# Causal self-attention of a four-layer kernel: the values of a head as the 32-column stationary operand, in bursts of four chunks, instead of the weights as a 128-column one

## The reference, cut to what matters

```python
h = _rms(x, n1_w)
heads = lambda w_: (h @ w_.T).reshape(B, T, HEADS, HD).transpose(0, 2, 1, 3)
q = _rms(heads(wq), qn_w);  k = _rms(heads(wk), kn_w);  v = heads(wv)
scores = jnp.einsum('bhqd,bhkd->bhqk', q, k) * HD ** (-0.5)
scores = jnp.where(causal[None, None], scores, -jnp.inf)
attn = jax.nn.softmax(scores, axis=-1)
ao = jnp.einsum('bhqk,bhkd->bhqd', attn, v).transpose(0, 2, 1, 3).reshape(B, T, C) @ wo.T
ao = ao.at[:, :, :M].set(0.0)
x = x + ao
```

## Time and profile before

| | |
|---|---|
| median of the runs | 1413.52 us (1412.07 to 1416.41, 3 runs) |
| profiled execution, own time | 1418.93 us |
| its span in the trace | 1417.1 us |
| TensorE matmul busy | 1156.5 us (82%) |
| TensorE weight loads busy | 943.7 us (67%) |
| VectorE busy | 935.8 us (66%) |
| ScalarE busy | 716.8 us (51%) |
| GpSimd busy | 582.7 us (41%) |

### The profile page before, as it was taken

One profiled execution on the slowest core, in us unless ns is written; L12 is line 12 of the kernel. 1 busy time (PEld: TensorE's weight loads), 2 busy tenths in 40 slices (PEclk: granted clock), 3 DMA queues, 4 the chain that ended last, 5 costly groups with the idle time before them and its releaser, 6 DMA issues. The chain is left out here.

```text
span 1417.1 us, 24304 instructions
## 1 busy us (share of the span) xinstructions
PE 1156.5 (82%) x6976; PEld 943.7 (67%) x6976; DVE 935.8 (66%) x2154; ACT 716.8 (51%) x1337; POOL 582.7 (41%) x588
## 2 busy tenths in 40 slices
PE   5978899998996899844999287359477499999997
PEld 2655688887884699843888155247356387878785
DVE  6657788885553577754665578547565676767775
ACT  3556666665543555442565266237353255555553
POOL 3316634341000232453333233436354166667664
PEclk9998999997997999965999699679777599999998
DMA  7999410100001300013110560122421263444443
GB/s 198 217 191 177 86 45 28 39 28 1 1 0 62 112 1 2 17 56 101 42 50 22 163 160 22 35 61 79 134 77 46 48 130 120 117 121 119 119 122 101
DMA packets 115311, 115.16 MB, mean 81 GB/s; under 512 B 17141, under 2 KB 82300, under 8 KB 115218
## 3 DMA queue, kind: packets, MB, share of 16 engines
q1 hardware_dynamic: 109250, 104.64, 31.4%
q0 software_dynamic: 4544, 8.47, 1.8%
q10 hardware_dynamic: 1424, 0.92, 0.2%
HBM read 74.44 MB, written 34.16 MB: 77 GB/s over the span
## 5 line engine op out<-in xcount | busy, mean ns | idle before, releaser
L3109 POOL TENSOR_TENSOR e_h<-e_h,e_gate 128x512 f32<-128x512 f32 x128 | 187.9, 1485 | 135.9 <-DVE e_h L3161 89.7
L3166 DVE TENSOR_TENSOR e_h_low<-e_h,e_h_high 128x512 fp32r<-128x512 f32 x132 | 117.5, 890 | 75.8 <-ACT e_h_high L3096 75.6
L3096 ACT ACTIVATE e_h_high<-e_h 128x512 fp32r<-128x512 f32 x132 | 83.5, 633 | 97.8 <-POOL e_h L3109 90.1
L2565 POOL DMA_INDIRECT sorted_y<-zT,e_zb x78 | 75.8, 972 | 128.8 <-DVE zT L2723 113.4
L3161 DVE TENSOR_TENSOR e_h<-e_s,e_ps_b 128x512 f32<-128x512 f32 x132 | 89.4, 678 | 13.2 <-ACT e_s L3081 9.0
L1716 PE MATMUL u_ps_o<-u_vaug,u_pT 128*128 128x72 f32 x768 | 97.7, 270 | 0.0
L550 POOL DMA_INDIRECT sorted<-w_rows,w_index x64 | 71.9, 1123 | 57.9 <-DVE w_index L456 28.0
L1716 PEld LDWEIGHTS u_ps_o<-u_vaug,u_pT 128*128 128x128 f32 x768 | 93.3, 192 | 0.9
L3081 ACT ACTIVATE e_s<-e_ps_a 128x512 f32<-128x512 f32 x132 | 77.8, 589 | 30.9 <-PE e_ps_a L2157 28.3
L1397 POOL TENSOR_TENSOR s_kbd<-s_keys,groupmask 96x512 fp32r<-96x512 f32 x64 | 65.2, 1039 | 59.7 <-DMA s_keys<-s_k 33.8
L1744 ACT ACTIVATE u_sm<-u_sm 128x512 f32<-128x512 f32 x96 | 60.5, 631 | 50.3 <-DVE u_sm L1772 49.7
(11 more groups left out here) (575 smaller groups left out, 3532.4 us busy)
## 6 DMA issues: line engine op xcount, KB each, us to landing
e_gate<-gates_by_expert SPq DMA_DIRECT2D x256, 128.0 KB, 3.1
sorted<-blank SPq DMA_DIRECT2D x2, 8775.0 KB, 77.9
a_q<-q_part SPq DMA_DIRECT2D x24, 256.0 KB, 6.9
w_raw<-in_L1w SPq DMA_DIRECT2D x24, 256.0 KB, 4.1
e_zb<-sorted SPq DMA_DIRECT2D x78, 65.0 KB, 1.8
w_rows<-sorted_y SPq DMA_DIRECT2D x16, 256.0 KB, 4.9
s_keys<-s_k SPq DMA_DIRECT2D x8, 384.0 KB, 3.5
s_qs<-s_q SPq DMA_DIRECT2D x16, 192.0 KB, 2.6
```

The lines of the kernel that those rows point to most:

```text
L2565: nc.gpsimd.indirect_dma_start(out=y_dram, out_offset=bass.IndirectOffsetOnAxis(ap=at, axis=0), in_=y[j % NY][:, :], in_offset=None, bound ...
L3096: nc.scalar.activation(h_parts[k % 3][0][:, :], h[k % 3][:, :], ACT.Copy).then_inc(high_ready, 1)
L3109: nc.gpsimd.tensor_tensor(h[c % 3][:, :], h[c % 3][:, :], gate[pair % SLOTS][:, :], ALU.mult)\
L3166: nc.vector.tensor_tensor(h_parts[k % 3][1][:, :], h[k % 3][:, :], h_parts[k % 3][0][:, :], ALU.subtract).then_inc(low_ready, 1)
```

## The change

The values of one head, padded to 32 columns (8 channels, a one, zeros), become the stationary operand and the transposed weights `pT` of a block the moving one (128 columns). Head h writes output partitions 32 x (h mod 4) and following, columns 128 x (h div 4) and following, of `ps_o`. The products of four chunks (a set of 16 blocks) are issued together, at steps 6, 10 and 2 of the next batch, so `pT` becomes a ring of six. The result is now channels x queries, so ScalarE copies the bank (`oT`, 128x512), TensorE turns it back in four transposes two steps on, and VectorE divides what comes back. The finishing steps move on by three, and the loop has eleven steps behind it instead of eight.

```diff
-    NA = 8 * HD + 8
     CH = 12
+    SET = 4
+    RING = 6
+    WIDE = 32
-        vaug = [m.sb(f"vaug{i}", [P, 2, 8 * (NA + HD)]) for i in range(2)]
+        vaug = [m.sb(f"vaug{i}", [P, HEADS, WIDE]) for i in range(2)]
-        pT = [m.sb(f"pT{i}", [P, 4, P]) for i in range(2)]
-        rden = m.sb("rden", [P, 2, 8])
+        pT = [m.sb(f"pT{i}", [P, 4, P]) for i in range(RING)]
+        oT = m.sb("oT", [P, 4 * P])
+        rden = m.sb("rden", [P, HEADS])
...
-        NORMALISE = {7: 0, 15: 1}
-        TURN = {8: 0, 16: 1}
-        PROJECT = {10: 0, 18: 1}
-        ADD = {11: 0, 19: 1}
+        def in_strips(first):
+            every = [(h, kb, c % RING, col // P) for c in range(first, first + SET) for h, kb, col in blocks(c)]
+            return sorted(every, key=lambda block: (block[0] // 4, block[1], block[0]))
+        def sets_done(b, c):
+            return b * (CH // SET) + c // SET + 1
+        COPY = {7: 0, 15: 1}
+        BACK = {9: 0, 17: 1}
+        NORMALISE = {10: 0, 18: 1}
+        TURN = {11: 0, 19: 1}
+        PROJECT = {13: 0, 21: 1}
+        ADD = {14: 0, 22: 1}
+        LAST = 11
...
-                wait(pool, pv_done, b * CH)
+                wait(pool, pv_done, b * (CH // SET))
...
-                if alive(n, 3):
+                if alive(n, 3) and (r - 3) % SET == SET - 1:
                     pe.wait_ge(pT_ready, n - 2)
                     c = (r - 3) % CH
+                    first, batch_at = c - SET + 1, b if r >= 3 else b - 1
                     par = 0 if c < 4 else 1
-                    if c in (0, 4):
-                        pe.wait_ge(v_ready, b * 2 + par + 1)
-                        wait(pe, on_ready, b * 2 + par - 1)
-                    for i, (h, kb, col) in enumerate(blocks(c)):
-                        a, own = h // 8, h % 8
-                        last = nc.tensor.matmul(ps_o[par][:, a * NA:(a + 1) * NA], pT[(r - 3) % 2][:, i, :],
-                                                vaug[kb][:, a, own * NA:(own + 1) * NA],
-                                                start=own == 0 and kb == 0, stop=own == 7 and kb == par)
+                    pe.wait_ge(v_ready, batch_at * 2 + par + 1)
+                    if first in (0, 4):
+                        wait(pe, on_ready, batch_at * 2 + par - 1)
+                    for h, kb, ring, col in in_strips(first):
+                        strip, cols = slice(h % 4 * WIDE, (h % 4 + 1) * WIDE), slice(h // 4 * P, (h // 4 + 1) * P)
+                        last = nc.tensor.matmul(ps_o[par][strip, cols], vaug[kb][:, h, :], pT[ring][:, col, :],
+                                                start=kb == 0, stop=kb == par, skip_group_check=True)
                     last.then_inc(pv_done, 1)
+                if found := finishing(BACK, r, b):
+                    par, tile = found
+                    pe.wait_ge(oT_out, tile + 1)
+                    for g in range(HEADS // HG):
+                        last = nc.tensor.transpose(ps_o[par][:, g * P:(g + 1) * P], oT[:, g * P:(g + 1) * P], ident)
+                    last.then_inc(o_back, 1)
...
                 if alive(n, 2):
                     act.wait_ge(t_done, n - 1)
-                    wait(act, pv_done, n - 3)
-                    nc.scalar.activation(pT[r % 2][:, :, :].rearrange("p a b -> p (a b)"), ps_t[r % 2][:, :],
+                    wait(act, pv_done, sets_done(b, r - 2 - RING))
+                    nc.scalar.activation(pT[(r - 2) % RING][:, :, :].rearrange("p a b -> p (a b)"), ps_t[r % 2][:, :],
                                          ACT.Copy).then_inc(pT_ready, 1)
...
+                if found := finishing(COPY, r, b):
+                    par, tile = found
+                    act.wait_ge(pv_done, sets_done(b if r == 7 else b - 1, 0 if par == 0 else CH - 1))
+                    wait(act, o_back, tile)
+                    nc.scalar.activation(oT[:, :], ps_o[par][:, :], ACT.Copy).then_inc(oT_out, 1)
...
                 if found := finishing(NORMALISE, r, b):
                     par, tile = found
-                    dve.wait_ge(pv_done, (b if r == 7 else b - 1) * CH + (4 if par == 0 else CH))
+                    dve.wait_ge(o_back, tile + 1)
                     wait(dve, ot_done, tile)
-                    halves = ps_o[par][:, 0:2 * NA].rearrange("p (a c) -> p a c", c=NA)
-                    nc.vector.reciprocal(rden[:, :, :], halves[:, :, 8 * HD:NA])
+                    heads = ps_o[par][:, :].rearrange("p (h c) -> p h c", c=WIDE)
+                    nc.vector.reciprocal(rden[:, :], heads[:, :, HD])
                     dve.drain()
-                    nc.vector.tensor_tensor(on[:, :].rearrange("p (a h d) -> p a h d", a=2, d=HD),
-                                            halves[:, :, 0:8 * HD].rearrange("p a (h d) -> p a h d", d=HD),
-                                            rden[:, :, :].unsqueeze(3).broadcast_to([P, 2, 8, HD]), ALU.mult)\
+                    nc.vector.tensor_tensor(on[:, :].rearrange("p (h d) -> p h d", d=HD), heads[:, :, 0:HD],
+                                            rden[:, :].unsqueeze(2).broadcast_to([P, HEADS, HD]), ALU.mult)\
                         .then_inc(on_ready, 1)
```

More of the change, by code:

```diff
@@ L1588, in attend_self @@
         pool_zeroed = m.sem("pool_zeroed")
-        (zeroed, far_ready, v_ready, s_done, sub_done, p_ready, t_done, pT_ready, pv_done, on_ready,
+        (zeroed, far_ready, v_ready, s_done, sub_done, p_ready, t_done, pT_ready, pv_done, oT_out, o_back, on_ready,
          ot_done, onT_ready, w_done, x_done) = (m.sem(n) for n in (
              "zeroed", "far_ready", "v_ready", "s_done", "sub_done", "p_ready", "t_done", "pT_ready",
-             "pv_done", "on_ready", "ot_done", "onT_ready", "w_done", "x_done"))
+             "pv_done", "oT_out", "o_back", "on_ready", "ot_done", "onT_ready", "w_done", "x_done"))
         block = stack.enter_context(nc.Block())
@@ L1643, in place_values @@
             def place_values(b, kb):
-                out = vaug[kb][:, :, :].rearrange("p a (h c) -> p (a h) c", c=NA + HD)[:, :, 0:HD]
+                out = vaug[kb][:, :, 0:HD]
                 src = v_all[:, bass.ds(b * 2 + kb, 1), :].rearrange("p a (h d) -> p (a h) d", d=HD)
@@ L1731, in _ @@
             keep_busy(nc, ps_w, ones_b, 8)
-            rotate_chunks(pe, step, 8)
+            rotate_chunks(pe, step, LAST)
         @block.scalar
@@ L1749, in step @@
                     nc.scalar.activation(onT[:, :], ps_w[:, 0:P], ACT.Copy).then_inc(onT_ready, 1)
-            rotate_chunks(act, step, 8)
+            rotate_chunks(act, step, LAST)
         @block.vector
@@ L1758, in _ @@
             for kb in range(2):
-                ones = vaug[kb][:, :, 0:8 * (NA + 1)].rearrange("p a (h c) -> p a h c", c=NA + 1)
-                last = nc.vector.memset(ones[:, :, :, 8 * HD:8 * HD + 1], 1.0)
+                last = nc.vector.memset(vaug[kb][:, :, HD:HD + 1], 1.0)
             last.then_inc(zeroed, 1)
@@ L1793, in step @@
                                        x2[:, bass.ds(tile, 1), :].rearrange("p a b -> p (a b)"))
-            rotate_chunks(dve, step, 8)
+            rotate_chunks(dve, step, LAST)
 class TwoWayScores:
```

## The result

The changed kernel takes 1393.9 us (median of four runs, 1392.13 to 1395.42) against 1412.8 before (four runs, 1407.04 to 1416.41): ratio 0.987, 95% interval 0.9834 to 0.9905, 18.9 us less. On another chip, later, it took 1396.06 against 1416.24 (ratio 0.9855, interval 0.9833 to 0.9877). The forecast was 15.8 us less, 1398 us, and a range of 1391 to 1408. The profiled execution took 1392.13 us by its own time, its span is 1390.3.

The account below looks back on a forecast made before the run. TensorE was taken as the bound at 1.76 us a chunk. Moving it to VectorE saves 20.2, less 3.2 for exposed bursts and 1.2 at the end: 15.8 us from 1413.5, about 1398 us, range 1391 to 1408.

Parts of the forecast that it names:

- TensorE was the bound, VectorE would be: Self-attention stage: TensorE sets the pace at 1.76 us a chunk; after the change VectorE does at 1.57.
- The sum of 1.20 us a chunk for TensorE: TensorE's predicted work per chunk after the change, scores, transposes, value products, ways in and out and finishing work included.
- Four strips stream at once, 0.11 us a group: Value products: four passes in different output strips take 0.11 us together, so a set of 32 passes takes 0.87 us.
- The rivals with 0.216 us a group and with no overlap: Value products: set of 1.73 us, 1410 us total, chance 0.05; or set of 3.5 us, 1450 total, chance 0.03.
- 0.2 us for the ways in and out: TensorE entering and leaving a burst of value products: 0.2 us a set for both, bounds 0.14 and 0.3.
- A drain of 0.42 us at each change: Full TensorE drain at each tiling mode change: 48 changes would cost TensorE 20 us, more than half of it covered.
- The end, 1.2 us longer: From the last subtraction's start to the last statistics' start: 7.4 us instead of 6.28.
- The exposure of the bursts, 3.2 us: Next scores stand behind each burst on TensorE: 0.3 at step 6 plus 0.1 a batch, eight batches, 3.2 us given back.
- the floor of 147.4: VectorE's unhindered stage time: 95 distances of 1.36 us plus 18.0 for divisions and additions, against 167.6 before.
- late by up to 0.45: ScalarE at step 6, delayed by the copy of step 3; 0.3 us was left there for it.
- ScalarE's copy is covered: New PSUM copy, 0.59 us a tile, fits in 2.4 us a batch spare; rival, exposed: 1404 to 1407 us, chance 0.12.
- The clock: Rival: the granted clock falls to 1.2 GHz as TensorE idles, about 1470 us if throughout; chance 0.04.

Follow-up runs that it names:

- the same edit to VectorE: Row maximum over half of each head's columns: kernel before, 1415.61 us against 1416.86; changed kernel, 1384.63 us against 1416.86.
- the kernel that comes nearest to no overlap: Changed kernel with a set's blocks ordered one output strip after the other: 1426.84 us against 1415.82 for the kernel before.
- the kernel without shift: Changed kernel without VectorE's row maximum and subtraction, ScalarE taking the exponential from PSUM: 1379.76 us against 1416.86 for the kernel before.

## Why the prediction was right, and where a size was off

- *TensorE was the bound, VectorE would be.* Shown from both sides: the same edit to VectorE gives 1.6 us in the loop before the change and 11.1 after it. The sum of 1.20 us a chunk for TensorE was 0.08 too low, since scores and transposes are 0.88 between starts of matmuls and not 0.80; with VectorE at 1.57 nothing hung on it.
- *Four strips stream at once, 0.11 us a group.* Shown by the stretches of one burst (0.81 us from first to last start of the 32 passes) and by the order of blocks, which alone costs 26 us in the loop. The rivals with 0.216 us a group and with no overlap are out; the kernel that comes nearest to no overlap is slower than before, though by 11 us and not by 37.
- *0.2 us for the ways in and out.* 2 x 0.09 measured. A drain of 0.42 us at each change is refuted.
- *The end, 1.2 us longer.* Measured 1.2.
- *The exposure of the bursts, 3.2 us.* The mis-sized term: 0.5 was measured (147.9 against the floor of 147.4), which is 2.7 of the 3 us between 15.8 and 18.9. Of the 3.2, 0.8 were for the loop head (eight batches of 0.1); the maxima across it are 1.36 apart like any others, so it cost nothing. The other 2.4 (eight of 0.3) came from ScalarE being "late by up to 0.45" at step 6; the exponentials of that step start 0.03 us behind the end of their subtractions, so it was not late at all. ScalarE was costed by the durations of its records, 0.631 and 0.593, where the distances of starts are 0.54 and 0.48. Its batch is 12 x 1.02 + 2 x (0.48 + 0.16) = 13.5 us and not 16.4, and it is 0.13 us late at step 4 and 0.29 at step 8, as 1.02 + 0.48 and 1.02 + 0.48 + 0.16 against VectorE's 1.36 say (0.14 and 0.30). The prediction had read TensorE and VectorE by starts, and this engine by durations. The Trainium skill, "ScalarE: Activation LUTs" (What ACT_TABLE_LOAD costs), says that back-to-back ACTIVATEs overlap by about 93 ns; the trace agrees, 0.63 us long and 0.54 apart for the exponential.
- *ScalarE's copy is covered.* True for one copy, and only just: the second was exposed to four fifths. The prediction's reason, room in the sum over a batch, would have covered the second as well.
- *The clock.* Full over the whole loop, with matmul records over 93% of it.

## What to carry to other kernels

A float32 product with at most 32 output rows can be made the stationary side and put into four strips of output partitions; order the blocks so that neighbours lie in different strips, and gather enough of them for all four strips to be in use. Entering and leaving the form costs 0.2 us a set, which mattered little here: sets of two chunks were within 1.8 us of sets of four in the loop, sets of one, with half of their strips empty in two thirds of the chunks, were 16.3 behind. When the bound moves to another engine, read that engine's floor from starts in a stretch in which it does not wait, and look at each step for what the other engines have queued ahead of it, not at sums over a batch. Once an engine is the bound, its drains are worth removing: putting the finishing work around a drain that is there anyway, and dropping two a tile, gave 5 us here.

## What the runs showed of the hardware

- Passes of different strips overlapped only where they were issued near each other: with eight passes of one strip before the next strip's, the new strip's first four ran beside the last four of the old (2.18 us for 32 passes, against 1.27 with two strips in turn, 0.81 with four, and 3.4 if 0.109 were paid for each).
- An ACTIVATE of 128x512 lasts 0.58 to 0.64 us in the changed kernel's trace, and the next starts 0.48 us behind it where it reads PSUM (copies, and the exponential of the kernel without shift) and 0.52 to 0.54 where it reads SBUF.
- A switch into the form with 32 stationary columns costs 0.09 us and a switch out of it 0.09 (0.203 us between starts instead of 0.11). The first weights behind it begin to load with their matmul (199.37 both, at the scores behind a burst), where those of transposes run 0.11 ahead (174.55 and 174.66 in the kernel with sets of one); that this is the reason is not shown.
